# Both 1x1 convolutions of the second stage in the basis where the eight permutations are block diagonal

## The chip, the cores and the metric

The kernel runs on one core of one Trainium2 chip. The metric is the time of the program on the device in microseconds (us), the median of three runs. All arithmetic is in 32-bit floats.

## The reference, cut to what matters

Input x is 16 images of 512 channels, 64 by 64. Layer 0 adds to x a 4x4 blur of its group-normalised self. Layer 1, which the change is about, normalises again and computes an involution with weights that depend on the position:

```python
def d4_1x1(x, w):                       # x: (b, cin*8, h, w), w: (cout, cin, 8)
    W = jnp.stack([w[..., jnp.array(p)] for p in PERMS], axis=1)
    xr = x.reshape(b, cin, 8, h, ww)
    return jnp.einsum('ogif,bifhw->boghw', W, xr).reshape(b, cout * 8, h, ww)

def layer1(x, w_v, w1, gn_gamma, gn_beta, w2, b2):
    t = relu(group_norm(d4_1x1(x, w1), gn_gamma, gn_beta, cmid))     # 512 -> 256 channels
    wgt = einsum('oi,bighw->boghw', w2, t.reshape(b, 32, 8, h, w)) + b2   # 9 taps x 4 groups x 8
    # taps of each of the 8 group elements are rotated or flipped
    xv = d4_1x1(x, w_v)                                              # 512 -> 512 channels
    pats = unfold_patches(xv, 3)                                     # 9 shifted copies
    return (wgt * pats).sum(over the 9 taps)

x = x + layer1(_gn(x), ...)
```

PERMS holds the eight permutations of the symmetries of a square. A layer `d4_1x1` is a full matrix over channels (512 by 512 and 512 by 256), built of 8 by 8 blocks that all have this permutation structure. In a suitable basis of the eight components such a block splits into four one-dimensional parts and two equal 2 by 2 parts.

## The kernel before

The first stage (`stage_a`) blurs all images, writes the sum `x1` to HBM and leaves a scale and a bias per channel and image (`x1_scale`, `x1_bias`). The second stage (`stage_b`) works on one image at a time. Its work order is written out by hand for each engine's queue and joined by semaphores; every queue runs in order.

An image is cut into 4 bands of 16 rows, and these into 4 units of 4 rows. A unit is done in 4 granules of 4 output channels for each of the 32 channel lines, so an image has 16 granules (`N_GRAN`), and `period(i)` walks over them with n = 0 to 15. In granule n:

- DVE multiplies the tap weights of the unit with shifted windows of `val` (`product`): taps 0 to 2 are summed by DVE itself with the residual in `acc` (`opening`, two halves; its last sum is L1015), taps 3 to 8 (`pooled`, products j = 0 to 5, the last two "late", within the next granule's opening) go to `prod_p`, a ring of four.
- POOL adds the six products to `acc`, one after the other (L917). Before a granule's first add it waits for DVE's sums in `acc` (`own`). After granule 13's adds it also does a power for the next image's statistics (`RSTD_AT`).
- SP loads the residual of granule n + 2 and stores `acc` of granule n - 1 once POOL has finished it.
- PE and ACT make `val` for granule n + 3 (`values`, `keep_values`): 1x1 convolution `w_v`, four input blocks (`kt`) by four bands as 32-column matmuls (L672), into a ring of two PSUM banks that ACT empties (`take`).
- At the end of a unit PE computes the tap weights of the next one into five other PSUM banks (`tap_weights`, L686): banks 0 to 2 "EARLY" after step 3, 7 or 11, banks 3 and 4 "LATE" at the start of step 4, 8 or 12. Each bank waits until DVE has read the old weights (`bank_done`), and ACT adds the bias (`tap_bias`, L823) before DVE may use it.

Between these the next image is prepared: SP loads its channels into `xm` (and the last unit into `xs`), ACT normalises them in place (`normalize`, L769), PE convolves them with `w1` in full 128-column matmuls of 512 pixels (`conv_t`, L656, at the steps in `CONV_AT`), ACT keeps the result `t`, DVE takes its statistics (`t_stats`, `t_aggregate`, at granules 6, 8, 10 and 12; `t_spreads`, `t_add_eps` and `t_affine` at 14), and ACT applies them with a relu. `rows_above` and `complete` copy the rows that bands share. After granule 15 comes `lead(i + 1)`: the first values, the relu of unit 0 and its tap weights. For the first image none of this lies under another's pooling; the last image has no next one to prepare (`more=False`).

Of the kernel before, what the change touches and what calls it, by code (L numbers as in the profile page):

```python
# [28 lines left out]
P = 128  # L29
# [61 lines left out]
def program(nc, x, shifts, mean_a, kern, member_of, w1t, wvt, w2t, w2mask, b2t, gamma, beta, mean_b, out, x1):  # L91

    with ExitStack() as top:
# [9 lines left out]
        with ExitStack() as ctx:  # L103
            stage_b(nc, ctx, sem, ps, x1, w1t, wvt, w2t, w2mask, b2t, gamma, beta, mean_b, out, x1_scale, x1_bias)
# [344 lines left out]
def stage_b(nc, ctx, sem, ps, x1, w1t, wvt, w2t, w2mask, b2t, gamma, beta, mean_b, out, x1_scale, x1_bias):  # L449
# [5 lines left out]
    xs = sb("xs", [P, KT, BANDS * UPX])  # L455
# [6 lines left out]
    w1 = sb("w1", [P, KT, CMID])  # L462
    wv = sb("wv", [P, KT, CM * 32])
# [16 lines left out]
    w1_in, const_in = sem("w1_in"), sem("b_const_in")  # L480
# [3 lines left out]
    xm_loaded = [sem(f"xm_loaded{u}") for u in range(UNITS)]  # L484
    xm_ready = sem("xm_ready")
    xs_ready = sem("xs_ready")
    xm_above = sem("xm_above")
    xm_whole = sem("xm_whole")
# [23 lines left out]
    LEAD_MM = 4 * UNITS + sum(V_BANKS[:AHEAD])  # L512
    PERIOD_MM = 4 * UNITS + sum(V_BANKS)

    CONV_AT = {1: (3, 0), 2: (0, 0), 4: (0, 1), 5: (3, 1), 6: (1, 0), 8: (1, 1), 10: (2, 0), 11: (2, 1)}
# [8 lines left out]
    def values_end(i, n, more=True):  # L524

        if n < AHEAD:
            return period_base(i) - sum(V_BANKS[n + 1:AHEAD])
        return period_base(i) + sum(V_BANKS[AHEAD:n + 1]) + \
            (2 * sum(s < n - AHEAD for s in CONV_AT) if more else 0)

    def t_end(i, u):

        if isinstance(i, int) and i == 0:
            return 4 * (u + 1)
        last = max(step for step, (unit, _) in CONV_AT.items() if unit == u)
        return period_base(i) - PERIOD_MM + sum(V_BANKS[AHEAD:last + AHEAD + 1]) + 2 * sum(x <= last for x in CONV_AT)

# [26 lines left out]
    def xs_rows(kt):  # L564
        return xs[:, kt, :].rearrange("p (q n) -> p q n", q=BANDS)
# [4 lines left out]
    def _(sp):  # L570
        def load_xm(i, u):
            if u == UNITS - 1:
                if not first(i):
# [180 lines left out]
    def _(act):  # L754
# [92 lines left out]
        for u in range(UNITS):  # L847
            if u == 0:
                normalize(0, 0)
# [284 lines left out]
```

## Time and profile before

| what | value |
|---|---|
| median of 3 runs | 5242.5 us (5240.94 to 5243.19) |
| the profiled execution, its own time | 5241.05 us |
| its span, first to last instruction | 5239.3 us |
| PE, DVE, ACT, POOL busy, share of the span | 88%, 89%, 45%, 86% |
| mean granted TensorE clock | 0.956 |
| PE in `values` (L672), `conv_t` (L656), tap weights (L686) | 2112.9, 692.8 + 227.9, 570.2 us |
| POOL adds (L917) | 3652.7 us, 1536 of 2378 ns |

"Busy" is the time with an instruction in work on the engine. Matmuls are pipelined, so PE's busy time and the mean of one matmul overstate what a single one costs in a row; the length of a burst divided by its instructions is the better price. An f32 matmul appears as two instructions. The shares are averages over both stages: the first ends near 1087 us. DVE and POOL rows that follow one another overlap by a little, so a row of starts says more than a sum of durations.

### The profile page before, as it was taken

What the parts mean: (1) busy time and instruction counts of PE and PEld (TensorE: products, weight loads), DVE (VectorE), ACT (ScalarE), POOL (GpSimd) and SP (SyncE); (2) the same over time, 40 slices, a digit from 0 to 9 for tenths busy, and PEclk for the clock granted to TensorE, in tenths of its full rate; (3) what the DMA queues carried; (4) which work ended last, traced back from release to release, by engine and by line L of the source; (5) the groups of instructions that cost most, each with busy time, mean ns of one, the idle gap of its engine ahead of it and who ended that gap; (6) DMA issues with size and microseconds to landing.
All of it is one profiled execution on the core that took longest, in us unless ns stands there. A gap on an engine that the chain in (4) does not pass through costs nothing.

```text
span 5239.3 us, 140780 instructions
## 1 busy us (share of the span) xinstructions
PE 4611.1 (88%) x52820; PEld 2173.0 (41%) x52820; DVE 4657.8 (89%) x7999; ACT 2349.3 (45%) x3633; POOL 4515.2 (86%) x2208
## 2 busy tenths in 40 slices
PE   8999999979898989898989898989898988888873
PEld 3333333334443434353435343434344444444342
DVE  6777777727999999999999999999999999999998
ACT  7999999944242333333333333333323233323221
POOL 6888888826998989898989898989898999899999
PEclk9999999989999999999999999999999999999986
DMA  8999999843333333232333333333333232323221
GB/s 237 257 257 257 257 257 257 235 129 103 100 102 101 99 98 115 85 119 91 111 98 103 101 98 102 102 98 102 98 102 114 86 117 83 114 95 109 82 74 57
DMA packets 868592, 681.28 MB, mean 130 GB/s; under 512 B 555840, under 2 KB 818368, under 8 KB 851520
## 3 DMA queue, kind: packets, MB, share of 16 engines
q1 hardware_dynamic: 868032, 673.64, 43.3%
q8 instruction: 373, 6.11, 0.5%
q14 instruction: 187, 1.53, 0.1%
HBM read 405.08 MB, written 268.44 MB: 129 GB/s over the span
## 4 chain that ended last, share of the span: by engine, by line
PE 37%; DVE 19%; issue 12%; POOL 6%; ACT 4%; DVEq 1%; DMA 0%; ACTq 0%; POOLq 0%; SPq 0%
PE ps L672 18%; PE ps L656 13%; PE ps L686 7%; POOL acc L917 6%; DVE prod_p L968 6%; DVE ps L1009 3%; DVE ps L1012 2%; DVE ps L968 2%; DVE acc L1015 2%; DVE prod_d L968 2%; DVE six_t L933 2%; ACT xs L769 1%; ACT t L830 1%; ACT val L817 1%; DVE dev_t L949 1%
## 5 line engine op out<-in xcount | busy, mean ns | idle before, releaser
L917 POOL TENSOR_TENSOR acc<-acc,prod_p 128x1024 f32<-128x1024 f32 x1536 | 3652.7, 2378 | 383.1 <-DVE acc L1015 156.2
L672 PE MATMUL ps<-xm,wv 128*32 128x256 f32 (+1 forms) x32768 | 2112.9, 418 | 121.4 <-ACT val L817 89.8
L968 DVE TENSOR_TENSOR prod_p<-ps,val 128x1024 f32<-128x1024 f32 x1536 | 1858.4, 1217 | 65.8 <-POOL acc L917 63.1
L672 PEld LDWEIGHTS ps<-xm,wv 128*32 128x32 f32 x32768 | 1070.3, 112 | 1165.2 <-issue 557.0
L284 PE MATMUL ps<-xn,band 64*64 64x512 f32 x8192 | 948.2, 598 | 21.5 <-issue 13.9
L817 ACT ACTIVATE val<-ps 128x512 f32<-128x512 f32 (+1 forms) x640 | 345.6, 556 | 1326.7 <-PE ps L672 1038.0
L968 DVE TENSOR_TENSOR prod_d<-ps,val 128x512 f32<-128x512 f32 x1024 | 698.8, 682 | 146.5 <-ACT ps L823 142.5
L656 PE MATMUL ps<-xm,w 128*128 128x512 f32 x1536 | 692.8, 605 | 88.3 <-ACT val L817 69.0
L686 PE MATMUL ps<-t,w 128*32 128x256 f32 x9216 | 570.2, 404 | 227.2 <-ACT t L830 117.6
L316 POOL TENSOR_TENSOR x_out<-x_out,x_in 128x512 f32<-128x512 f32 x512 | 636.2, 1274 | 0.0
L244 ACT ACTIVATE x_out<-ps 64x512 f32<-64x512 f32 x1024 | 606.2, 592 | 50.5 <-PE ps L284 29.1
L686 PEld LDWEIGHTS ps<-t,w 128*32 128x32 f32 x9216 | 302.4, 116 | 496.2 <-DVE ps L1009 117.2
L284 PEld LDWEIGHTS ps<-xn,band 64*64 64x64 f32 x8192 | 326.3, 132 | 432.3 <-issue 428.0
L656 PEld LDWEIGHTS ps<-xm,w 128*128 128x128 f32 x1536 | 287.9, 192 | 457.2 <-issue 377.8
L331 POOL TENSOR_TENSOR rstd<-var_eps,power 128x8 f32 (+2 forms) x133 | 212.9, 1601 | 237.3 <-DVE var_eps L378 237.3
L823 ACT ACTIVATE ps<-ps,b 128x256 f32<-128x256 f32 x576 | 235.1, 443 | 403.5 <-PE ps L686 401.1
L231 ACT ACTIVATE xn<-x_in,norm_b,rstd 128x512 f32<-128x512 f32 x512 | 389.5, 809 | 6.7
L798 ACT ACTIVATE t<-ps 128x512 f32<-128x512 f32 x192 | 114.6, 597 | 563.1 <-PE ps L656 563.1
L1009 DVE TENSOR_TENSOR ps<-ps,acc 128x512 f32<-128x512 f32 x512 | 353.8, 691 | 10.8 <-DMA acc<-x 10.8
L1012 DVE TENSOR_TENSOR ps<-ps,prod_d 128x512 f32<-128x512 f32 x512 | 353.8, 691 | 0.0
L968 DVE TENSOR_TENSOR ps<-ps,val 128x512 f32<-128x512 f32 x512 | 353.7, 691 | 0.0
L1015 DVE TENSOR_TENSOR acc<-ps,prod_d 128x512 f32<-128x512 f32 x512 | 349.4, 682 | 0.0
(59 smaller groups left out, 2366.8 us busy)
## 6 DMA issues: line engine op xcount, KB each, us to landing
x_in<-x SPq DMA_DIRECT2D x128, 1024.0 KB, 7.4
x<-x_out SPq DMA_DIRECT2D x256, 512.0 KB, 5.3
acc<-x SPq DMA_DIRECT2D x1024, 128.0 KB, 2.7
out<-acc SPq DMA_DIRECT2D x256, 512.0 KB, 2.7
xm<-x SPq DMA_DIRECT2D x192, 512.0 KB, 5.9
xs<-x SPq DMA_DIRECT2D x64, 512.0 KB, 6.4
wv<-wvt SPq DMA_DIRECT2D x1, 1024.0 KB, 8.0
w<-w1t SPq DMA_DIRECT2D x1, 512.0 KB, 8.2
```

Source lines behind the costliest of these rows:

```text
L244: nc.scalar.activation(group(x_out[H2 * t:H2 * t + H2, r, :], W, W, 0, 2 * two + x).rearrange("p m h w -> p m (h w)"), ps[at:at + H2, 2 * ...
L284: mm = nc.tensor.matmul(ps[to:to + H2, 2 * two + t, :], band[rows, v, rows], group(xn[rows, k % N_RING, :], XP, W, v, 2 * two + x), start= ...
L316: nc.gpsimd.tensor_tensor(out, out, group(x_in[:, k % X_RING, :], W, W, 0, g) .rearrange("p m h w -> p m (h w)"), ALU.add).then_inc(x_adde ...
L656: mm = nc.tensor.matmul(ps[:, b, :], w1[:, kt, m * P:(m + 1) * P], rows[:, 2 * h:2 * h + 2, :], start=(kt == 0), stop=(kt == KT - 1))
L672: mm = nc.tensor.matmul(ps[32 * q:32 * q + 32, b, at:at + ROWS[u] * W], wv[:, kt, (m + x) * 32:(m + x + 1) * 32], xm[:, kt, r0:r0 + ROWS[u ...
L686: mm = nc.tensor.matmul(taps_of(tap)[32 * q:32 * q + 32, :], w2[:, kt, tap * 32:(tap + 1) * 32], t[:, kt, u, q * UPX:(q + 1) * UPX], start ...
L817: nc.scalar.activation(val[:, m:m + per, lo:lo + ROWS[u], 1:1 + W], src, ACT.Copy) .then_inc(kept, 1)
L917: nc.gpsimd.tensor_tensor(acc[:, r, :], acc[:, r, :], prod_p[:, k % P_RING, :], ALU.add).then_inc(p_added, 1)
L968: return nc.vector.tensor_tensor(dst.rearrange("p (m r w) -> p m r w", m=count, w=W), taps_of(tap).rearrange("p (m r w) -> p m r w", m=1, ...
L1009: nc.vector.tensor_tensor(ps[:, D_BANK, :], ps[:, D_BANK, :], acc[:, r, half], ALU.add).then_inc(own, 1)
L1012: nc.vector.tensor_tensor(ps[:, D_BANK, :], ps[:, D_BANK, :], prod_d[:, 0, :], ALU.add).then_inc(own, 1)
L1015: nc.vector.tensor_tensor(acc[:, r, half], ps[:, D_BANK, :], prod_d[:, 1, :], ALU.add).then_inc(own, 1)
```

## The change

Both convolutions are computed in the basis in which the permutation structure is block diagonal. An image is cut into 8 chunks of 512 pixels (half a unit). For a chunk, `forward` transforms the four input blocks of 128 channels into four `xh` tiles, each of one irreducible part; normalisation is applied when ACT evicts them (`keep_forward`, with a scale and bias carried into the new basis by `affine`). `block_v` and `block_t` multiply with the block matrices `wh` for the two convolutions; their results, still in the new basis, go to `xm` and `t`. `inverse` transforms `t` back, in place; for the other convolution the back transform is what `values` now does, with one matmul per band instead of four. The chunks' steps have tables of their own. Raw input goes to `xr`, a buffer of one chunk. `wh` is built on DVE at the start of the stage. The bands' shared rows are copied by `edges`. DVE's statistics move to granules 5, 8, 11 and 13.

```diff
-LOAD_AT = {1: 0, 5: 1, 9: 2}
-LOAD_LAST_AT = 15
-NORMALIZE_AT = {2: 0, 6: 1, 10: 2}
-ABOVE_AT = 9
+IRR = 4
+CHUNKS, CPX = 8, 512
+OQ = QM + MT
+FORWARD_AT = {0: 0, 1: 1, 2: 2, 4: 3, 6: 4, 7: 5, 8: 6, 9: 7}
+BLOCK_V_AT = {1: 0, 2: 1, 4: 2, 5: 3, 8: 4, 9: 5, 12: 6, 13: 7}
+BLOCK_T_AT = {1: (0,), 2: (1,), 4: (2,), 5: (3,), 8: (4,), 9: (5,), 10: (6, 7)}
+INVERSE_AT = {1: (0,), 2: (1,), 4: (2,), 5: (3,), 8: (4,), 9: (5,), 11: (6, 7)}
+LOAD_AT = {1: 1, 2: 2, 3: 3, 5: 4, 7: 5, 8: 6, 9: 7}
+LOAD_NEXT_AT = 10
+EDGES_AT = 13
 RSTD_AT = (13, 5)
-WHOLE = 2
+EDGES = 2
 SETUP = 4
...
     block = ctx.enter_context(nc.Block())
...
-        def load_xm(i, u):
...
-                wait_apart(sp, sp_apart, mm_full, values_end(i - 1, GRANS * u + GRANS - 1))
+        def load_x(i, c):
+
+            if not (first(i) and c == 0):
+                prev = (i, c - 1) if c > 0 else (i - 1, CHUNKS - 1)
+                wait_apart(sp, sp_apart, mm_full, chunk_end(prev[0], "forward", prev[1]))
...
+                sp.dma_start(xr[:, kt, :].rearrange("p (q n) -> p q n", q=2), src).then_inc(x_loaded, 16)

...
+        sp.dma_start(base[:], basis).then_inc(base_in, 16)
+        load_x(0, 0)
+        sp.dma_start(w_src, wsrc).then_inc(w_in, 16)
+        sp.dma_start(w_sign, signs).then_inc(w_in, 16)
+        for dst, src in ((w2, w2t), (blk, mean_b), (b2, b2t), (gam, gamma), (bet, beta)):
             sp.dma_start(dst[:], src).then_inc(const_in, 16)
         sp.dma_start(mask, w2mask).then_inc(const_in, 16)
...
+        for c in range(1, CHUNKS):
+            load_x(0, c)
         load_resid(0, 0)
         load_resid(0, 1)
-        load_xm(1, UNITS - 1)
+        load_x(1, 0)

...
                 if more and n in LOAD_AT:
-                    load_xm(i + 1, LOAD_AT[n])
-                if ahead and n == LOAD_LAST_AT:
-                    load_xm(i + 2, UNITS - 1)
+                    load_x(i + 1, LOAD_AT[n])
+                if ahead and n == LOAD_NEXT_AT:
+                    load_x(i + 2, 0)
...
-        def conv_t(i, u, halves):
...
+        def affine():
+
+            for kt in range(KT):
+                q = slice(32 * kt, 32 * kt + 32)
+                nc.tensor.matmul(ps[q, D_BANK, 0:B], first_of,
+                                 x1_scale[:].rearrange("p (b k) -> p k b", k=KT)[:, kt, :], start=True, stop=True,
+                                 skip_group_check=True)
+                for r in range(IRR):
+                    mm = nc.tensor.matmul(ps[q, D_BANK, (1 + r) * B:(2 + r) * B], forward_m[:, r, :],
+                                          x1_bias[:].rearrange("p (b k) -> p k b", k=KT)[:, kt, :],
+                                          start=True, stop=True, skip_group_check=True)
+            mm.then_inc(affine_mm, 1)
+
+        def forward(i, c):
+
+            pe.wait_ge(x_loaded, i * (16 * KT * CHUNKS) + 16 * KT * (c + 1))
+            for r in range(IRR):
+                b = take()
+                for kt in range(KT):
+                    mm = nc.tensor.matmul(ps[32 * kt:32 * kt + 32, b, :], forward_m[:, r, :], xr[:, kt, :],
+                                          start=True, stop=True, skip_group_check=True)
+                mm.then_inc(mm_full, 1)
+
+        def block_of(i, c, outputs):
+
+            pe.wait_ge(kept, chunk_end(i, "forward", c))
+            for o in outputs:
+                b = take()
+                for r in range(IRR):
+                    mm = nc.tensor.matmul(ps[32 * r:32 * r + 32, b, :], wh[:, r, o, :], xh[:, c % 2, r, :],
+                                          start=True, stop=True, skip_group_check=True)
+                mm.then_inc(mm_full, 1)
+
+        def block_v(i, c):
+            block_of(i, c, range(QM))
+
+        def block_t(i, c):
+            block_of(i, c, range(QM, OQ))
+
+        def inverse(i, c):
+
+            pe.wait_ge(kept, chunk_end(i, "block_t", c))
+            for m in range(MT):
+                b = take()
+                nc.tensor.matmul(ps[:, b, :], inverse_t, t_chunk(m, c), start=True, stop=True).then_inc(mm_full, 1)

         def values(n, halves=(0, 1)):

-            u, m0 = n // GRANS, n % GRANS * QM
+            u, q4 = n // GRANS, n % GRANS
             per = QM // V_BANKS[n]
-            for m in range(m0 + halves[0] * QM // 2, m0 + (halves[-1] + 1) * QM // 2, per):
+            for m in range(halves[0] * QM // 2, (halves[-1] + 1) * QM // 2, per):
                 b = take()
                 for x in range(per):

                     row, at = (0 if u == 0 else u * UR + 2), x * ROWS[u] * W
-                    for kt in range(KT):
-                        for q in range(BANDS):
-                            r0 = (q * BR + row) * W
-                            mm = nc.tensor.matmul(ps[32 * q:32 * q + 32, b, at:at + ROWS[u] * W],
-                                                  wv[:, kt, (m + x) * 32:(m + x + 1) * 32],
-                                                  xm[:, kt, r0:r0 + ROWS[u] * W],
-                                                  start=(kt == 0), stop=(kt == KT - 1), skip_group_check=True)
+                    for q in range(BANDS):
+                        r0 = (q * BR + row) * W
+                        mm = nc.tensor.matmul(ps[32 * q:32 * q + 32, b, at:at + ROWS[u] * W],
+                                              inverse_v[:, m + x, :], xm[:, q4, r0:r0 + ROWS[u] * W],
+                                              start=True, stop=True, skip_group_check=True)
                 mm.then_inc(mm_full, 1)
...
-            pe.wait_ge(xm_above, i + 1)
+            pe.wait_ge(xm_edges, EDGES * (i + 1))
...
+        pe.wait_ge(base_in, 16)
+        affine()
+        forward(0, 0)
+        pe.wait_ge(w_built, 1)
+        for c in range(CHUNKS):
+            block_v(0, c)
+            block_t(0, c)
+            if c < CHUNKS - 1:
+                forward(0, c + 1)
+            inverse(0, c)
+        pe.wait_ge(const_in, 16 * 6)
...
             for n in range(N_GRAN):
                 if n > 0 and n % GRANS == 0:
                     tap_weights(i, n // GRANS, LATE)
-                if n + AHEAD == 2 * GRANS:
-                    pe.wait_ge(xm_whole, WHOLE * (i + 1))
                 if n + AHEAD < N_GRAN:
                     values(n + AHEAD)
-                if more and n in CONV_AT:
-                    u, half = CONV_AT[n]
-                    conv_t(i + 1, u, [half])
+                if more:
+                    if n in BLOCK_V_AT:
+                        block_v(i + 1, BLOCK_V_AT[n])
+                    for c in BLOCK_T_AT.get(n, ()):
+                        block_t(i + 1, c)
+                    if n in FORWARD_AT:
+                        forward(i + 1, FORWARD_AT[n])
+                    for c in INVERSE_AT.get(n, ()):
+                        inverse(i + 1, c)
                 if n % GRANS == GRANS - 1 and n < N_GRAN - 1:
                     tap_weights(i, n // GRANS + 1, EARLY)
             if more:
...
+        def keep_forward(i, c):
+
+            for r in range(IRR):
+                b = take(apart=True)
+                nc.scalar.activation(xh[:, c % 2, r, :], ps[:, b, :], ACT.Identity,
+                                     bias=xh_affine[:, 1 + r, bass.ds(i, 1)],
+                                     scale=xh_affine[:, 0, bass.ds(i, 1)]).then_inc(kept, 1)
+
+        def keep_block_v(i, c):
+
+            for q4 in range(QM):
+                b = take()
+                nc.scalar.activation(xm_chunk(q4, c), ps[:, b, :].rearrange("p (q n) -> p q n", q=2), ACT.Copy)\
+                    .then_inc(kept, 1)
+
+        def keep_block_t(i, c):
+
+            if c >= CHUNKS - 2 and not first(i):
+                act.wait_ge(t_ready, i * (MT * UNITS))
+            for m in range(MT):
+                b = take()
+                nc.scalar.activation(t_chunk(m, c), ps[:, b, :], ACT.Copy).then_inc(kept, 1)
+
+        def keep_inverse(i, c):
+
+            for m in range(MT):
+                b = take()
+                nc.scalar.activation(t_chunk(m, c), ps[:, b, :], ACT.Copy).then_inc(kept, 1)
+
+        def edges(i):
...
             if not first(i):
                 act.wait_ge(mm_full, values_end(i - 1, N_GRAN - 1))
...
+            act.wait_ge(kept, chunk_end(i, "block_v", CHUNKS - 1))
+            nc.scalar.activation(bands[:, :, 1:, 0:W], bands[:, :, 0:BANDS - 1, (BR - 2) * W:(BR - 1) * W], ACT.Copy)\
+                .then_inc(xm_edges, 1)
+            nc.scalar.activation(bands[:, :, 0:BANDS - 1, (BR - 1) * W:], bands[:, :, 1:, W:2 * W], ACT.Copy)\
+                .then_inc(xm_edges, 1)
...
-            keep_t(0, u, range(MT))
-            if u == UNITS - 2:
-                rows_above(0)
+        act.wait_ge(affine_mm, 1)
+        nc.scalar.activation(xh_affine[:], ps[:, D_BANK, 0:(1 + IRR) * B].rearrange("p (e b) -> p e b", b=B), ACT.Copy)\
+            .then_inc(affine_kept, 1)
+        act.wait_ge(affine_kept, 1)
+        keep_forward(0, 0)
+        for c in range(CHUNKS):
+            keep_block_v(0, c)
+            keep_block_t(0, c)
...
                 t_add_eps(i + 1)
             pooled(i, n, 2)
-            if more and n == 6:
+            if more and n == 5:
                 t_stats(i + 1, 0)
             if more and n == 8:
+                t_stats(i + 1, 1)
+            if more and n == 11:
+                t_stats(i + 1, 2)
+            pooled(i, n, 3)
+            if more and n == 13:
                 t_stats(i + 1, 3)
-            if more and n == 10:
-                t_stats(i + 1, 1)
-            pooled(i, n, 3)
-            if more and n == 12:
-                t_stats(i + 1, 2)
                 t_aggregate(i + 1)
             if more and n == 14:
                 t_affine(i + 1)
...
-        dve.wait_ge(const_in, 16 * 7)
+        dve.wait_ge(w_in, 32)
+        w_sum = ps[:, 0:2, 0:4 * OQ * 16].rearrange("p b (c o) -> p b c o", c=4)
+        for j in range(GR):
+            if j > 1:
+                dve.wait_ge(w_chain, 2 * j - 1)
+            coeff = w_src[:, j, :].rearrange("p (b c o) -> p b c o", b=1, c=1).to_broadcast([P, 2, 4, OQ * 16])
+            sign = w_sign[:, j].rearrange("p b (c o) -> p b c o", o=1).to_broadcast([P, 2, 4, OQ * 16])
+            nc.vector.tensor_tensor(w_term if j > 0 else w_sum, coeff, sign, ALU.mult).then_inc(w_chain, 1)
+            if 0 < j < GR - 1:
+                dve.wait_ge(w_chain, 2 * j)
+                nc.vector.tensor_tensor(w_sum, w_sum, w_term, ALU.add).then_inc(w_chain, 1)
+        dve.wait_ge(w_chain, 2 * GR - 2)
+        for b in range(2):
+            for e in range(2):
+                def part(a):
+                    return a[:, b].rearrange("p (r e) (q o) -> p r e q o", e=2, o=16)[:, :, e]
+                last = nc.vector.tensor_tensor(wh[:, 2 * b:2 * b + 2, :, 16 * e:16 * e + 16],
+                                               part(w_sum), part(w_term), ALU.add)
+        last.then_inc(w_built, 1)
+        dve.wait_ge(const_in, 16 * 6)
```

Left out of the diff: names of semaphores and tiles, the index helpers that count the order of the ring (`chunk_end` gives the number of evictions up to the end of a chunk's step), and the host's preparation of the transform matrices, the signs and the coefficients `wsrc`.

## Rows read from the trace of the kernel before

**Rows 1.** Windows: busy us (instructions) of PE, PEld, DVE, ACT, POOL; granted clock, DMA
```profile
2241.60:2494.10 252.50, 222.58 (x2758) 109.72 (x2757) 241.18 (x316) 84.65 (x131) 230.14 (x98) 0.96 0.32 102
2450.50:2458.40 7.90, 7.67 (x100) 3.92 (x104) 7.59 (x10) 1.73 (x5) 5.83 (x3) 0.69 0.25 89
5018.80:5239.30 220.50, 109.91 (x1700) 63.13 (x1688) 191.70 (x244) 28.62 (x57) 204.60 (x87) 0.74 0.18 63
```

**Rows 2.** Waits in one image: engine, waited for, us, times, longest
```profile
DVE prod_d L968 <- ACT ps L823: 7.8, 6, 3.7
...
POOL acc L917 <- DVE acc L1015: 8.0, 4, 2.3
...
DVE prod_p L968 <- POOL acc L917: 3.0, 3, 1.1
```

**Rows 3.** Waits of DVE in the last image, all of them
```profile
DVE prod_p L968 <- POOL acc L917: 16.8, 16, 1.3
```

**Rows 4.** DVE timeline at granule 4: start, us, instruction, idle before
```profile
2268.07 0.69 DVE L968 TENSOR_TENSOR prod_d<-ps,val 128x512 f32<-128x512 f32 x1 [3.70 <-ACT ps L823]
...
2269.79 0.69 DVE L968 TENSOR_TENSOR prod_d<-ps,val 128x512 f32<-128x512 f32 x1 [0.43 <-ACT ps L823]
```

**Rows 5.** POOL timeline of one image, the adds after its longest waits
```profile
2280.61 105.82 POOL L917 TENSOR_TENSOR acc<-acc,prod_p 128x1024 f32<-128x1024 f32 x42 [2.34 <-DVE acc L1015]
...
2436.51 0.71 POOL L904 TENSOR_TENSOR rstd_t<-var_eps_t,power_b 128x2 f32<-128x2 f32 x1 [1.19 <-DVE var_eps_t L955]
...
2454.03 75.65 POOL L917 TENSOR_TENSOR acc<-acc,prod_p 128x1024 f32<-128x1024 f32 x30 [1.93 <-DVE acc L1015]
```

**Rows 6.** POOL timeline of the last image: six adds a granule
```profile
5025.26 14.88 POOL L917 TENSOR_TENSOR acc<-acc,prod_p 128x1024 f32<-128x1024 f32 x6 [0.17 <-POOL acc L917]
...
5055.43 15.04 POOL L917 TENSOR_TENSOR acc<-acc,prod_p 128x1024 f32<-128x1024 f32 x6 [0.17 <-POOL acc L917]
...
5221.32 14.77 POOL L917 TENSOR_TENSOR acc<-acc,prod_p 128x1024 f32<-128x1024 f32 x6 [0.17 <-POOL acc L917]
```

**Rows 7.** Chain that ended last, one image: PE bursts and small DVE work
```profile
2244.28 7.04 PE ps L672 x128
2251.32 7.06 PE ps L656 x16
...
2405.37 2.39 DVE six_t L933 x4
...
2428.40 1.93 DVE dev_t L949
```

**Rows 8.** Lines of one image by form: ACT rows and one DVE row
```profile
L968 DVE TENSOR_TENSOR prod_p<-ps,val 128x1024 f32<-128x1024 f32 x97 | 117.4, 1217 | 3.2 <-POOL acc L917 3.0
...
L769 ACT ACTIVATE xm<-xm,x_bias,x_scale 128x1024 f32<-128x1024 f32 x12 | 13.9, 1232 | 0.0
...
L798 ACT ACTIVATE t<-ps 128x512 f32<-128x512 f32 x12 | 7.2, 598 | 35.6 <-PE ps L656 35.6
...
L789 ACT ACTIVATE xm<-xs 128x4096 f32<-128x4096 f32 x1 | 3.6, 3614 | 0.0
```

**Rows 9.** Lines of the whole run: ACT normalisation of the first stage
```profile
L231 ACT ACTIVATE xn<-x_in,norm_b,rstd 128x512 f32<-128x512 f32 x512 | 389.5, 809 | 6.7
```

**Rows 10.** Chain that ended last, start of the second stage
```profile
1089.20 7.50 DMA xm<-x
...
1101.58 57.92 PE ps L656 x128
1159.50 10.46 PE ps L672 x128
...
1175.46 9.60 PE ps L686 x144
```

**Rows 11.** POOL timeline of the first image: granules 0 and 4
```profile
1190.36 15.01 POOL L917 TENSOR_TENSOR acc<-acc,prod_p 128x1024 f32<-128x1024 f32 x6 [17.94 <-DVE acc L1015]
...
1274.88 15.00 POOL L917 TENSOR_TENSOR acc<-acc,prod_p 128x1024 f32<-128x1024 f32 x6 [3.24 <-DVE acc L1015]
```

More of the change, by code:

```diff
@@ L511, in stage_b, with order_of_period, order_at_first, ends @@
     EARLY, LATE = (0, 1, 2), (3, 4)
-    LEAD_MM = 4 * UNITS + sum(V_BANKS[:AHEAD])
-    PERIOD_MM = 4 * UNITS + sum(V_BANKS)
-    CONV_AT = {1: (3, 0), 2: (0, 0), 4: (0, 1), 5: (3, 1), 6: (1, 0), 8: (1, 1), 10: (2, 0), 11: (2, 1)}
+    LEAD = sum(V_BANKS[:AHEAD])
+    def order_of_period(more):
+        for n in range(N_GRAN):
+            if n + AHEAD < N_GRAN:
+                yield ("values", n + AHEAD), V_BANKS[n + AHEAD]
+            if more:
+                if n in BLOCK_V_AT:
+                    yield ("block_v", BLOCK_V_AT[n]), QM
+                for c in BLOCK_T_AT.get(n, ()):
+                    yield ("block_t", c), MT
+                if n in FORWARD_AT:
+                    yield ("forward", FORWARD_AT[n]), IRR
+                for c in INVERSE_AT.get(n, ()):
+                    yield ("inverse", c), MT
+    def order_at_first():
+        yield ("forward", 0), IRR
+        for c in range(CHUNKS):
+            yield ("block_v", c), QM
+            yield ("block_t", c), MT
+            if c < CHUNKS - 1:
+                yield ("forward", c + 1), IRR
+            yield ("inverse", c), MT
+    def ends(order):
+        total, at = 0, {}
+        for what, n in order:
+            total += n
+            at[what] = total
+        return at, total
+    IN_PERIOD, PERIOD_MM = ends(order_of_period(True))
+    IN_LAST, _ = ends(order_of_period(False))
+    AT_FIRST, FIRST_MM = ends(order_at_first())
+    LEAD_MM = FIRST_MM + LEAD
+    PERIOD_MM += LEAD
     def taps_of(tap):
@@ L527, in values_end, with chunk_end @@
             return period_base(i) - sum(V_BANKS[n + 1:AHEAD])
-        return period_base(i) + sum(V_BANKS[AHEAD:n + 1]) + \
-            (2 * sum(s < n - AHEAD for s in CONV_AT) if more else 0)
+        return period_base(i) + (IN_PERIOD if more else IN_LAST)["values", n]
+    def chunk_end(i, what, c):
+        if isinstance(i, int) and i == 0:
+            return AT_FIRST[what, c]
+        return period_base(i) - PERIOD_MM + IN_PERIOD[what, c]
     def t_end(i, u):
[L533 to L536, printed above, removed]
+        return chunk_end(i, "inverse", 2 * u + 1)
     def p_done(i, n, j):
@@ L762, in take @@
             return b
-        def normalize(i, u):
-            wait_apart(act, act_apart, xm_loaded[u], (i + 1) * (16 * KT))
-            for kt in range(KT):
-                v, done = (xs_rows(kt), xs_ready) if u == UNITS - 1 else (xm_rows(kt, u), xm_ready)
-                nc.scalar.activation(v, v, ACT.Identity, bias=x1_bias[:, bass.ds(i * KT + kt, 1)],
-                                     scale=x1_scale[:, bass.ds(i * KT + kt, 1)]).then_inc(done, 1)
-        bands = xm[:].rearrange("p k (q n) -> p k q n", q=BANDS)
@@ L860, in _ @@
         keep_values(0, 2)
-        complete(0)
         relu(0, 1)
```

164 lines of the change are left out of this document (76 added, 88 removed).

## The prediction

> **What bounds the kernel now.** I read the windows first. Of one image in the middle (252.5 us) VectorE (DVE) is busy 241.2, GpSimd (POOL) 230.1, TensorE (PE) 222.6, ScalarE (ACT) 84.7 [rows 1]. Three engines are near full, so shares decide nothing; the waits do. DVE waits in that image 7.8 us for ACT's bias on the tap weights and 3.0 us for POOL's adds, and for nothing else of size [rows 2]. The first sort is where PE matters: the tap weights of the next unit are queued on PE behind `values` and `conv_t`, and at granule 4 DVE stands still 3.70 us and then 0.43 us for them [rows 4].
>
> Next, what DVE would be held by if those waits went. POOL's 230 us understate it: its adds are chained, 42 of them take 105.82 us from first to last, so 2.52 us each and 15.12 us a granule of six [rows 5]. DVE's own work in a plain granule is shorter. The last image shows it: it has no convolutions of a next image, its granules follow each other at 15.08 us ((5221.32 - 5025.26) / 13) [rows 6], DVE never waits for ACT and waits 16.8 us in all for POOL, about 1.05 a granule [rows 3]. So DVE needs about 14.0 us, and POOL sets the pace wherever DVE is not held up. Sixteen granules at 15.12 are 241.9 us; that is the floor an image can come near. The time between the S4 marks (the first add of granule 4) of the first and last image is 5055.43 - 1274.88 over 15 images, 252.04 us each [rows 6, 11]. About 10 us an image are on offer, of which PE's lateness is only a part: POOL runs dry four times (8.0 us in all) waiting for DVE's sums [rows 2], 2.34 at granule 4 and 1.93 at granule 15, so 3.8 between, in granules 12 and 13, and 1.19 more at the small `rstd_t` power [rows 5]. Granule 15's is the price of DVE's small statistics operations, not of PE.
>
> **PE's part.** A 128x128 instruction of 512 columns takes 0.441 us (7.06 / 16), an instruction of a 32-column group with 256 columns 0.055 (7.04 / 128) [rows 7]; an f32 matmul is two instructions, so four 32-column groups of 512 columns, or one full matmul of 512, are 0.88 us. Per image that removes `conv_t` (128 instructions, 56.5 us) and three quarters of `values` (2048 instructions down to 512; of about 126 us, at 0.055 and 0.082 each [rows 7, 10], some 95 go). It adds 32 forward, 32 `block_v`, 16 `block_t` and 16 `inverse` fills of 0.88, 84.7 us. PE falls from 222.6 to about 156 us. For the four groups running together with 512 columns the rows of 256 speak; if they ran only two at a time a fill would be 1.76.
>
> **ACT's part.** Removed: 16 normalisations of 1.23 (19.7 us), the copy of 3.6 and two small ones, about 25 us. Added: 32 forward evictions with scale and bias, not seen before from PSUM: between 0.60 (a plain eviction [rows 8]) and 0.81 (scale and bias, SBUF to SBUF [rows 9]); I take 0.75, nearer the form with both pointers, 24 us. Then 32 `block_v` and 16 `block_t` evictions at 0.60, 29 us, and two edge copies of about 0.8. ACT goes from 85 to about 115 us (bounds 110 to 117): not a bound. PE fills one bank (0.88) while ACT empties the other (0.60 to 0.75), so the ring runs at PE's pace.
>
> **Does the new order keep the tap weights in time?** Of DVE's 14.0 us in a granule six products take about 1.13 each back to back (1.217 less their overlap [rows 8]), so the twelve short operations 0.6. `val` of granule n - 1 is thus free 5.2 us into granule n (five short ones and two late products), and there ACT's step n begins. A full step (1, 2, 4, 8, 9) has 14 fills or fewer, 12 of them 0.88, about 13 us with a halo copy; it ends before the next step opens. Steps 3, 7 and 11, which end in the early tap weights, hold two values fills and none, four or four chunk fills: PE is through at about 7, 10.5 and 10.5 us. Bank 0 is released by DVE at 7.1 (three short ones more); its 32 instructions (1.76) and two biases end near 10, 13 and 13 us, before granule end at 15.1. So the waits at granules 4, 8 and 12 go; a small one stays at granule 0, behind the relu. Loads: `xr` is a single buffer, a chunk's load starts when the forward of the chunk before is done and SP has stored the granule before. For chunk 5 that puts landing (at most 7.5 us, the row of the first load [rows 10]) about 6 us into granule 7, where PE wants it; PE waits in order, so lateness there moves the tap weights behind it, but some 2 us are covered by slack. Residual loads and stores queue behind SP's new waits; they are needed a granule later.
>
> **DVE's part in the loop.** The same four statistics groups (2.39 us each [rows 7]) move; the last, with its aggregation, comes in granule 13, directly before the small operations of 14, one of which takes 1.93 [rows 7]. DVE can be behind POOL's pace by what the wait of 4.13 us at granule 4 cost POOL less: 4.13 - 2.34, 1.8 us [rows 4, 5]. After the group of granule 11 that cover is 1.8 + 1.05 - 2.39 = 0.5; one plain granule makes it 1.5; then granule 13's 3.0 and the first small operations' 2.2 against another 1.05 leave POOL dry by 2.7 us, plus 0.8 for the power behind it. Granule 15's 1.93 stays (1.8 beyond the usual hand-over). New image: 241.9 + 3.5 + 1.8 = 247.2 us, against 252.04: 4.8 saved. For leftovers of tap waits I give back 0.5: 4.3 x 15 = 65 us.
>
> **The start.** No chunk work hides behind pooling in the first image. Before, convolutions take 57.92 us from 1101.58, `values` 10.46, statistics and relu up to 1175.46 [rows 10]. After: sources of the block matrices land near 1100; DVE builds them in 14 chained operations of 768 elements, about 0.95 each (a product of 1024 takes 1.22 [rows 8]) and four short ones, to about 1115.5. Then 92 fills at 0.88 with some hand-over, 84 us, to 1199.5; edges 1.7; `values(0)` a quarter, 2.6; the same 5.5 us of statistics and relu: tap weights start at 1209.5, 34 us later. POOL's first add moves from 1190.36 to 1224. From there granules run at 15.1, since the residual load that had to wait behind a load for image 1 no longer does, and no convolution delays granule 4: S4 comes at 1284.7 instead of 1274.88 [rows 11]. Net cost 10 us.
>
> **Sum.** 5239.3 + 10 - 65 = 5184 us of span; the profiled run has 1.75 us outside its span and lies 1.5 below the median, so 5187; I state 5185.
>
> **The rivals.** (1) PE's lower clock, slower than before. In the stretch 2450.5 to 2458.4, behind a wait for ACT, the granted clock is 0.69, a mean of 1.2 and 2.4 GHz, and the 96 tap instructions cost 7.67 us of PE instead of 5.3 [rows 1, 7]. With PE idle a third of the time, steps 7 and 11 open cold; if their four fills (7.0 us from 6.4) and the taps (3.5 a bank) run at 1.2 GHz, bank 0 is ready at 17.8 us and bank 1 at 21.3, and DVE waits 5.0 us at granule 8 and 3.7 at 12. By the same cover sum an image loses 8.1 and takes 255.3: 5239 + 10 + 49, about 5298. It decides from about 3.5 us of wait at each. Against it: in the last image the clock is 0.74 and DVE waits for no bias at all [rows 1, 3]. The Trainium skill speaks for this rival: "TensorE: Matmul & The Clock Gate", HAM oscillation, says that pauses between bursts put the array back to half clock, so fewer matmuls need not be less time; the row at 0.69 agrees. (2) Half of that: only step 11's lateness counts, about 2.5 us an image back: 5184 + 30, 5215. A late chunk load gives about the same. (3) Fill and eviction do not overlap, 1.2 us a fill: start 92 x 0.32 = 29 us longer, 5215 with a little from heavy steps running over. The skill's "TensorEngine Tiling (Array Packing)", PSUM Bottleneck, warns of it: packing speeds up the array, not the emptying of PSUM. Evictions of 0.60 against fills of 0.88 say no. (4) The change doesn't save: POOL and DVE trade waits as before, the image stays at 252, and the start costs its 10: 5251.
>
> **How the numbers follow.** Forecast 0.60; (1) 0.08; (2) 0.14; (3) 0.10; (4) 0.08. 0.2% (10.5 us) is about what a measurement of this kernel tells from no change. Faster: the forecast, (2) and (3) less a small part, 0.81; same: (4) mostly, 0.09; slower: (1) and the rest, 0.10. The forecast's own range is 5150 (all tap waits gone, starving 1.5 us less than worked out, start 10 cheaper) to 5205; the range that takes in (2) and (3) goes to 5238.
>
> **What would show it.** In the profile after: PE near 156 us an image, ACT near 115; DVE's waits for the bias under 2 us an image and those for POOL up from 3 to about 7; the granules 15.1 apart except at 13 to 15; POOL's first add near 1224. Wrong would be: bias waits at granules 8 or 12 with the clock low; PE waiting for chunk loads in the loop; a chunk at the start far from 10.6 us; or POOL's adds slower than 2.52 us.

## The result, and the profile after

The changed kernel takes 5194.8 us (median of four runs, 5193.2 to 5196.2) against 5242.8 for the kernel before on the same chip: a ratio of 0.9909, 95% interval 0.9892 to 0.9926. The forecast was 5185, with 5150 to 5205 as its own range and 5238 as the end of the range that takes in rivals (2) and (3). The profiled execution has a span of 5193.5 us.

First the page after, the busy shares and the chain that ended last by engine, and below them that chain in the kernel before.

```profile
PE 3796.5 (73%) x36988; PEld 1315.4 (25%) x36988; DVE 4670.5 (90%) x8017; ACT 2854.0 (55%) x4642; POOL 4507.4 (87%) x2208
...
POOL 51%; DVE 13%; issue 9%; PE 4%; POOLq 1%; ACT 1%; DMA 0%; DVEq 0%; SPq 0%; ACTq 0%
```

```profile
PE 37%; DVE 19%; issue 12%; POOL 6%; ACT 4%; DVEq 1%; DMA 0%; ACTq 0%; POOLq 0%; SPq 0%
```

PE has gone from 88% of the span to 73%, but the shares of DVE and POOL are nearly what they were. What changed is the chain: half of it is now POOL's adds, and PE has 4% for 37%. Before, it ran through PE's bursts behind `values` and `conv_t` again and again [rows 7].

A window as the first of [rows 1], one image in the middle of the run:

```profile
1979.10:2226.90 247.80, 174.75 (x1764) 56.39 (x1764) 239.32 (x313) 115.92 (x194) 228.13 (x97) 0.86 0.33 103
```

The image has 1764 PE instructions for 2758, PE is busy 175 us for 223, ACT 116 for 85, and the granted clock fell from 0.96 to 0.86.

The waits of DVE and of POOL over the fifteen steady images (1230 to 5000 us), against those of [rows 2]:

```profile
DVE prod_p L1078 <- POOL acc L1027: 96.4, 109, 1.2
DVE prod_d L1078 <- ACT ps L929: 16.5, 32, 1.0
...
POOL rstd_t L1014 <- DVE var_eps_t L1065: 55.5, 15, 3.7
POOL acc L1027 <- DVE acc L1125: 50.4, 22, 18.1
```

DVE's wait for the bias on the tap weights is 1.1 us an image (16.5 / 15), from 7.8; no single one is longer than 1.0. Its waits for POOL have risen from 3.0 to 6.4 (96.4 / 15). POOL's own long waits are now two an image, 3.70 before the power and 1.94 before granule 15, which its timeline shows (start, duration, instruction, idle before):

```profile
1230.01 14.96 POOL L1027 TENSOR_TENSOR acc<-acc,prod_p 128x1024 f32<-128x1024 f32 x6 [18.07 <-DVE acc L1125]
...
1290.77 15.00 POOL L1027 TENSOR_TENSOR acc<-acc,prod_p 128x1024 f32<-128x1024 f32 x6 [0.17 <-POOL acc L1027]
...
2141.15 45.05 POOL L1027 TENSOR_TENSOR acc<-acc,prod_p 128x1024 f32<-128x1024 f32 x18 [0.23 <-POOL acc L1027]
2189.91 0.71 POOL L1014 TENSOR_TENSOR rstd_t<-var_eps_t,power_b 128x2 f32<-128x2 f32 x1 [3.70 <-DVE var_eps_t L1065]
2190.59 14.82 POOL L1027 TENSOR_TENSOR acc<-acc,prod_p 128x1024 f32<-128x1024 f32 x6
2207.35 181.35 POOL L1027 TENSOR_TENSOR acc<-acc,prod_p 128x1024 f32<-128x1024 f32 x72 [1.94 <-DVE acc L1125]
...
5010.19 14.86 POOL L1027 TENSOR_TENSOR acc<-acc,prod_p 128x1024 f32<-128x1024 f32 x6 [0.17 <-POOL acc L1027]
```

The hole of 2.34 us at granule 4 [rows 5] is gone: 72 adds, twelve granules, run without a stop at 2.52 us each (181.35 / 72). The S4 marks are 1290.77 and 5010.19, so an image takes 247.96 us (before 252.04). The books close: 15 x 4.08 = 61.2 us saved in the images, 15.9 lost before the first mark (1290.77 - 1274.88), and behind the last mark 183.3 us for 183.9. Together 5239.3 - 61.2 + 15.9 - 0.6 = 5193.4, the span.

Where the 15.9 come from, the chain at the start of the second stage shows (start, duration, what):

```profile
1109.67 1.16 DVE wh L1177 x4
1110.87 8.08 PE ps L732 x48
...
1125.03 5.51 PE ps L732 x48
1130.54 1.04 PE ps L722 x8
1131.69 0.79 ACT xh L871
1132.52 1.11 PE ps L722 x8
...
1134.66 1.96 PE ps L747 x4
1136.62 5.51 PE ps L732 x48
...
1205.12 4.37 PE ps L760 x32
...
1214.99 5.20 PE ps L773 x57
```

`wh` is built by 1110.87, and eight chunks take 92.5 us to the last eviction at 1203.40. A chunk is 11.59 us (1136.62 - 1125.03): six block fills in 5.51, the four forward fills with two of their evictions on the path, two inverse fills. Tap weights start at 1214.99 instead of 1175.46 [rows 10], POOL's first add at 1230.01 instead of 1190.36 [rows 11]; 24 of the 40 us come back by the S4 mark, since nothing holds granules 0 to 4 up any more.

### The profile page after: what moved, and what is told of

It is laid out like the page before. It is cut to its first block, busy times and chain, and to the rows that moved or that the text cites. A ratio compares the mean times of both kernels' runs of the same rounds, so it can differ in the third digit from the quotient of the medians.

```text
span 5193.5 us, 113938 instructions
## 1 busy us (share of the span) xinstructions
PE 3796.5 (73%) x36988; PEld 1315.4 (25%) x36988; DVE 4670.5 (90%) x8017; ACT 2854.0 (55%) x4642; POOL 4507.4 (87%) x2208
## 4 chain that ended last, share of the span: by engine, by line
POOL 51%; DVE 13%; issue 9%; PE 4%; POOLq 1%; ACT 1%; DMA 0%; DVEq 0%; SPq 0%; ACTq 0%
POOL acc L1027 51%; DVE prod_p L1078 3%; DVE ps L1122 2%; DVE ps L1119 2%; DVE ps L1078 1%; DVE six_t L1043 1%; DVE acc L1125 1%; DVE prod_d L1078 1%; PE ps L722 1%; PE ps L732 1%; PE ps L773 1%; DVE dev_t L1059 1%; POOLq L1024 1%; DMA xr<-x 0%; POOLq L1026 0%
## 5 line engine op out<-in xcount | busy, mean ns | idle before, releaser
L773 PE MATMUL ps<-t,w 128*32 128x256 f32 x9216 | 614.0, 425 | 435.7 <-ACT t L936 225.5
L760 PE MATMUL ps<-xm,base 128*32 128x256 f32 (+1 forms) x8192 | 636.2, 445 | 166.4 <-ACT val L923 73.7
L732 PE MATMUL ps<-xh,wh 128*32 128x512 f32 x6144 | 706.8, 600 | 49.6 <-ACT val L923 33.7
L722 PE MATMUL ps<-xr,base 128*32 128x512 f32 x4096 | 547.1, 659 | 213.3 <-ACT val L923 124.1
L871 ACT ACTIVATE xh<-ps,xh_affine 128x512 f32<-128x512 f32 x512 | 395.1, 777 | 195.5 <-PE ps L722 180.0
L879 ACT ACTIVATE xm<-ps 128x512 f32<-128x512 f32 x512 | 306.0, 598 | 190.4 <-PE ps L732 190.4
L760 PEld LDWEIGHTS ps<-xm,base 128*32 128x32 f32 x8192 | 251.2, 115 | 563.8 <-issue 186.4
L916 ACT ACTIVATE val<-val 128x512 f32<-128x512 f32 x192 | 120.5, 628 | 436.7 <-DVE prod_p L1078 436.6
```

Of the source, the lines that this page charges most:

```text
L722: mm = nc.tensor.matmul(ps[32 * kt:32 * kt + 32, b, :], forward_m[:, r, :], xr[:, kt, :], start=True, stop=True, skip_group_check=True)
L732: mm = nc.tensor.matmul(ps[32 * r:32 * r + 32, b, :], wh[:, r, o, :], xh[:, c % 2, r, :], start=True, stop=True, skip_group_check=True)
L760: mm = nc.tensor.matmul(ps[32 * q:32 * q + 32, b, at:at + ROWS[u] * W], inverse_v[:, m + x, :], xm[:, q4, r0:r0 + ROWS[u] * W], start=True ...
L773: mm = nc.tensor.matmul(taps_of(tap)[32 * q:32 * q + 32, :], w2[:, kt, tap * 32:(tap + 1) * 32], t[:, kt, u, q * UPX:(q + 1) * UPX], start ...
L871: nc.scalar.activation(xh[:, c % 2, r, :], ps[:, b, :], ACT.Identity, bias=xh_affine[:, 1 + r, bass.ds(i, 1)], scale=xh_affine[:, 0, bass. ...
```

## The experiments

The theory: the images gain because PE is no longer late with the tap weights, after which POOL's chained adds set the pace. Rivals: PE's lateness only changes places with POOL's waits; the lower clock takes the gain back; the gain is that of the moved statistics on DVE.

**Less PE work in the kernel before.** It leaves out three of the four input blocks of `values`, and nothing else: no transform, no moved statistics, no longer start.

```diff
-                    for kt in range(KT):
+                    for kt in range(1):
...
-                                                  start=(kt == 0), stop=(kt == KT - 1), skip_group_check=True)
+                                                  start=True, stop=True, skip_group_check=True)
```

> The kernel before, with the value convolution over the first of its four input blocks only (three of four blocks are left out, so 95 us less of PE an image and nothing else changed). Theory A, PE's lateness at the tap weights: DVE's waits for the bias fall from 9.0 us an image to under 1.5, POOL paces the loop, an image takes 246 to 248 us instead of 252.0, and the whole about 5150 us. Theory B, the gain came from the rest of the rearrangement (statistics moved, loads, evictions): within 0.2% of the kernel before, 5243. Theory C, a less busy PE drops to its lower clock and is late all the same: bias waits stay above 5 us an image and the time above 5215.

Measured: 5188.2 us, ratio 0.9893 (0.9876 to 0.9909): less than expected, and not where it was expected. The profiled span is 51.8 us shorter (5187.5 for 5239.3). About half of that, 24.9, lies ahead of the S4 mark of the first image (1249.93 for 1274.88): from 1175 to 1280 DVE waits 7.9 us for ACT and the residual's load instead of 35.5. The S4 marks then follow at 250.28 us instead of 252.04, 26 us over the run. POOL's timeline shows what became of its stops, and below it stands one stretch of the kernel before:

```profile
1675.32 180.56 POOL L917 TENSOR_TENSOR acc<-acc,prod_p 128x1024 f32<-128x1024 f32 x72 [1.93 <-DVE acc L1015]
...
1874.48 14.85 POOL L917 TENSOR_TENSOR acc<-acc,prod_p 128x1024 f32<-128x1024 f32 x6 [3.38 <-DVE acc L1015]
```

```profile
1448.25 181.54 POOL L917 TENSOR_TENSOR acc<-acc,prod_p 128x1024 f32<-128x1024 f32 x72 [1.76 <-DVE acc L1015]
```

The hole at granule 4 is gone in every image behind the first, but there is now one of 3.3 to 3.4 us at granule 12 of every image but the last, where the kernel before mostly has 1.7. POOL's waits come to 142.1 us from 1300 to 4900, against 144.9 before, so in the loop the lateness has moved more than it has gone. Most of the 26 us is POOL's pace instead: 72 adds in a row take 180.56 us for 181.54, which makes 1.3 us an image. Why the adds are a little faster with less work on PE, no run shows.

At granule 12 the clock bites. DVE's timeline at granule 12 (start, duration, instruction, idle before), and the chain of the same stretch:

```profile
2113.09 0.69 DVE L968 TENSOR_TENSOR prod_d<-ps,val 128x512 f32<-128x512 f32 x1 [5.64 <-ACT ps L823]
```

```profile
2100.17 10.14 PE ps L656 x16
```

In the kernel before, the same convolution of 16 instructions takes 7.06 us when PE is kept busy ahead of it [rows 7]. At the place shown it takes 7.13 there, behind a pause of PE of 2.15 us. Here the pause, in which PE waited for ACT's `val`, is 4.7 us, the granted clock from 2100 to 2112 is 0.74, a mean of 1.2 and 2.4 GHz, and the burst takes 10.14. The wait at granule 12 is then 5.64 us where the kernel before has 2.63. The waits for the bias fell only to 5.6 us an image (81.2 us from 1300 to 4900, for 117.8 before).

**The PE work put back into the changed kernel.** `values` does its matmuls three times, with the same result.

```diff
-                    for q in range(BANDS):
+                    for q in list(range(BANDS)) * 3:
```

> The changed kernel, with each matmul of the values done three times over (same result; about 63 us of PE an image added, which brings PE back to some 220 us, the load of before). Theory A: the tap weights are late again, bias waits of several us an image, an image takes 250 to 254 us instead of 248.0, the whole 5230 to 5290. Theory B: nothing changes, 5195.

Measured: 5300.8 us, ratio 1.0112 (1.0095 to 1.0129), slower than the kernel before. PE is busy 221.6 us of an image of 253.5 and the clock is back at 0.97. Behind the first image DVE waits 113.9 us for the bias (1330 to 4900), and POOL's hole at granule 4 is back in every image but the last:

```profile
2317.72 4.94 POOL L1027 TENSOR_TENSOR acc<-acc,prod_p 128x1024 f32<-128x1024 f32 x2 [0.95 <-DVE prod_p L1078]
2326.03 75.71 POOL L1027 TENSOR_TENSOR acc<-acc,prod_p 128x1024 f32<-128x1024 f32 x30 [3.37 <-DVE acc L1125]
```

The image is as the theory expected, and makes 84 of the 106 us over the changed kernel (15 times 253.54 - 247.96). The total is above the expectation, because POOL stood still 19 us more at granule 4 of the first image (15.89 and 3.25). PE at full clock and late costs more here than PE at 0.86 and in time.

**The statistics put back to granules 6, 8, 10 and 12** (the four numbers in `period` alone).

> The changed kernel, with DVE's statistics at granules 6, 8, 10 and 12 as in the kernel before. Theory A with the cover of 1.8 us: POOL runs dry by 0.1 us at granule 11, 1.0 at 13, 1.2 and the power at 14, 1.8 at 15; about half a microsecond an image less than now, 5187 us, within 15 of the changed kernel. Theory B, the moved statistics saved the time: 2 us an image or more given back, 5225 or above.

Measured: 5211.3 us, ratio 0.9939 (0.9923 to 0.9956), between the two expectations, and neither holds. The image is 249.2 us. Of the 48 us that the change gained, 16.5 hang on where the statistics are and about 32 on the rest; neither alone is the cause. POOL's timeline shows where, at granules 9 and 13, each right behind a group of statistics:

```profile
2363.07 29.98 POOL L1027 TENSOR_TENSOR acc<-acc,prod_p 128x1024 f32<-128x1024 f32 x12 [1.32 <-DVE acc L1125]
...
2426.10 14.84 POOL L1027 TENSOR_TENSOR acc<-acc,prod_p 128x1024 f32<-128x1024 f32 x6 [2.11 <-DVE acc L1125]
```

The expectation had no stop at granule 9 and 1.0 us at 13. The places also act on the tap weights: DVE's waits for the bias are 54.0 us (1300 to 4900), where the changed kernel has 16.5. So the two causes are not cleanly apart in this run.

**The statistics in halves.** If a group of 2.39 us is too much for the 1.05 us that DVE has over in a granule, two groups of half the size in neighbouring granules should let it keep up.

```diff
+STATS_AT = {5: (0, [0]), 6: (0, [1]), 7: (1, [0]), 8: (1, [1]), 10: (2, [0]), 11: (2, [1]), 12: (3, [0]), 13: (3, [1])}
...
+            if more and n in STATS_AT:
+                t_stats(i + 1, *STATS_AT[n])
```

> The changed kernel, with each unit's statistics cut in two halves in neighbouring granules (5 to 8 and 10 to 13), the aggregation at 13. Theory A with the cover of 1.8 us: a half costs 1.2 us where a granule gives back 1.05, so POOL reaches granule 14 with cover left; its wait there falls from 3.7 us to about 1.4, an image to 245.3 us, the whole to 5155 to 5165. If POOL's pace alone sets the loop, or its waits don't come from DVE's work in granules 11 to 13: no change, 5195.

Measured: 5151.5 us, ratio 0.9826 (0.981 to 0.9842), the image 245.2, both close to what was expected. POOL's wait at the power falls from 3.70 to 1.19; the one at granule 15 stays at 1.94.

**And DVE's small operations with an operand in PSUM.** What stays is the 1.19 and 1.94, and both follow operations on two numbers a partition (`dev_t`, `t_bias`) that take 2 us. In the changed kernel's rows by form, in the middle of the run:

```profile
L1074 DVE TENSOR_TENSOR t_bias<-bet,dev_t 128x2 f32<-128x2 f32 x1 | 2.3, 2257 | 0.0
L1059 DVE TENSOR_TENSOR dev_t<-dev_t 128x2 f32<-128x2 f32 x1 | 2.0, 1957 | 0.0
L1070 DVE TENSOR_TENSOR t_scale<-rstd_t,gam 128x2 f32<-128x2 f32 x1 | 0.9, 941 | 0.0
...
L1072 DVE TENSOR_TENSOR dev_t<-t_scale,ps 128x2 f32<-128x2 f32 x1 | 0.2, 156 | 0.0
```

The fast one reads PSUM, the slow ones SBUF alone. The edit keeps the deviation, its square and the product for the bias in a free corner of the PSUM bank that `opening` uses; for that it computes the deviation twice and waits for DVE's own sums. The diff is cut to two of the operations:

```diff
-            nc.vector.tensor_tensor(dev[:], dev[:], dev[:], ALU.mult).then_inc(t_chain, 1)
+            nc.vector.tensor_tensor(square_ps, dev_ps, dev[:], ALU.mult).then_inc(t_chain, 1)
...
-            nc.vector.tensor_tensor(t_bias[:], bet[:], dev[:], ALU.subtract).then_inc(t_norm, 1)
+            nc.vector.tensor_tensor(t_bias[:], bet[:], dev_ps, ALU.subtract).then_inc(t_norm, 1)
```

> The changed kernel with the split statistics of the run before, and two of DVE's three slow small operations at granule 14 given an operand in PSUM instead of SBUF only. Theory D: a small DVE operation whose operands all lie in SBUF waits until POOL's running add ends; then the square of 1.96 us and the bias of 2.26 us fall to about 0.2 each, POOL's waits at granules 14 and 15 (1.2 and 1.9 us) go, an image takes 242.5 us and the whole about 5112 us. Rival: these operations are slow for another reason, keep their time, and the whole stays at 5151.

Measured: 5114.5 us, ratio 0.9756 (0.974 to 0.9773), the image 242.84 (S4 marks at 1292.13 and 4934.73), as theory D expected: the best version of this study, faster than both kernels. The same rows, and POOL's timeline:

```profile
L1066 DVE TENSOR_TENSOR ps<-ps,dev_t 128x2 f32<-128x2 f32 x1 | 0.2, 168 | 0.0
...
L1082 DVE TENSOR_TENSOR t_bias<-bet,ps 128x2 f32<-128x2 f32 x1 | 0.2, 157 | 0.0
```

```profile
2204.53 166.26 POOL L1028 TENSOR_TENSOR acc<-acc,prod_p 128x1024 f32<-128x1024 f32 x66 [0.59 <-DVE acc L1134]
2371.01 45.13 POOL L1028 TENSOR_TENSOR acc<-acc,prod_p 128x1024 f32<-128x1024 f32 x18 [0.23 <-POOL acc L1028]
2416.40 0.71 POOL L1015 TENSOR_TENSOR rstd_t<-var_eps_t,power_b 128x2 f32<-128x2 f32 x1 [0.25 <-DVE var_eps_t L1073]
```

**Both DVE edits in the kernel before,** with PE's work as it was (the aggregation moves from granule 12 to 13).

> The kernel before with DVE's part of both runs alone: its statistics in halves at granules 6 to 13, the small operations by PSUM; PE's work as it was. Theory A: PE's lateness at granules 4 and 12 remains (DVE waits about 9 us an image for the bias, POOL runs dry some 2.3 and 1.3 us there), DVE's share of POOL's dry time goes; an image takes about 246.6 us, the whole 5155 to 5170. If PE's lateness were all that held the kernel before: no change, 5243. If DVE's own work were all: the time of the changed kernel with the same edits, less its longer start, near 5100.

Measured: 5153.8 us, ratio 0.9831 (0.9814 to 0.9847). The two small edits gain more on the old kernel (88 us) than the change of the convolutions (48). On top of them the change still brings 39 (5153.8 to 5114.5), so DVE's side work was not all that held the kernel before. With PE's work left in, DVE waits 93.1 us for the bias (1300 to 4900; 26.8 in the changed kernel with the same edits), and POOL has a hole of over 2 us at granule 4 in five of the fourteen images between the first and the last, here one of them:

```profile
2268.65 105.75 POOL L918 TENSOR_TENSOR acc<-acc,prod_p 128x1024 f32<-128x1024 f32 x42 [3.38 <-DVE acc L1024]
```

**A plain forward eviction.** It leaves out the scale and bias of the normalisation, to price the start's chunk.

```diff
-                nc.scalar.activation(xh[:, c % 2, r, :], ps[:, b, :], ACT.Identity,
-                                     bias=xh_affine[:, 1 + r, bass.ds(i, 1)],
-                                     scale=xh_affine[:, 0, bass.ds(i, 1)]).then_inc(kept, 1)
+                nc.scalar.activation(xh[:, c % 2, r, :], ps[:, b, :], ACT.Copy).then_inc(kept, 1)
```

> The changed kernel, with the forward evictions as plain copies (the scale and the bias of the normalisation are left out). Theory E: in the first image a forward's four fills wait for evictions of 0.78 us in the ring of two banks; with 0.60 they don't, a chunk takes 11.1 us instead of 11.6, POOL's first add comes about 4 us earlier, and the loop doesn't change. Rival: the fills themselves take 1.04 us, the chunk stays at 11.6.

Measured: 5189.6 us in a single run. The chain at the start:

```profile
1109.31 7.61 PE ps L732 x48
...
1122.63 5.51 PE ps L732 x48
1128.14 3.73 PE ps L722 x32
...
1131.90 1.96 PE ps L747 x4
1133.86 5.51 PE ps L732 x48
...
1144.65 6.12 DMA xr<-x
```

The evictions are off the chain and the chunk is 11.23 us instead of 11.59: of the 1.0 us above the forecast's 10.6 they are a third. The rest is the fills themselves, 0.92 to 0.98 us each (5.51 / 6, 3.73 / 4, 1.96 / 2) with PE at its upper level, a granted clock of 1.00, in that stretch of the changed kernel (1130.54 to 1190.47); 0.88 was taken. A faster chunk also runs into its load, which takes part of the gain back: the eight chunks take 91.0 us for 92.5. POOL's first add came 2.8 us earlier, at 1227.22, but 1.6 of that was there before the first chunk's block fills (1109.31 for 1110.87).

## Why the prediction was right, and where its sizes were off

**What bounds the kernel.** Right: with PE in time, POOL's adds set the pace at 2.52 us each, and the granules follow at 15.1. The lateness of the tap weights is shown as a cause by the PE work put back: bias waits, the hole at granule 4 and 5.6 us an image came back with it. Less PE work alone, in the kernel before, gave the image only 1.8 us, most of it by POOL's faster adds; there the waits did mostly change places, as rival (4) says. For the changed kernel that rival is refuted: POOL's waits are 87.3 us from 1300 to 4900 where the kernel before has 144.9. That granule 12 is in time as well follows from its trace, but no run takes apart which part of the new order does it.

**Where POOL runs dry.** Right in place, nearly in size, and that in part by luck. At granule 14, 2.7 + 0.8 = 3.5 us were forecast; the gap beyond the usual hand-over is 4.2 (2190.59 - 2186.20 - 0.17). At granule 15 it is 1.8, as forecast (1.94 - 0.17). With the floor of 241.9 that is 247.9, the measured image but for 0.06. The 0.5 given back for late tap weights came to less than that: the image shown here has one hole of 0.71 at granule 9, the next none. So 0.7 too little at granule 14 and most of the 0.5 cancel, and the image was mis-sized by 0.26 us (247.96 for 247.7), 4 us in all. The account behind the 3.5, that DVE can be 1.8 us behind before POOL runs dry, did not hold with the statistics at their old places: there it gave 5187, and 5211.3 was measured, with waits for the bias that it left out. What the cover really is, no run measures.

**ACT and PE.** ACT's 115 us came out as 115.9, the forward eviction at 0.777 us for the 0.75 taken. PE is busy 175 us, not 156. Busy overstates, and the clock was lower; the two can't be told apart here. Neither made DVE wait more than 1.1 us an image for the bias.

**The start** is the term that was off most: the S4 mark at 1290.77 for 1284.7, 6.1 us. `wh` was ready 4.6 us sooner than worked out, mostly because DVE could begin at 1095.85 and not near 1100. Against that, eight chunks cost 92.5 us instead of 84: 2.6 in the first burst, which followed a pause of PE and took 8.08 us at a granted clock of 0.67 where later ones take 5.51; the rest in fills of 0.92 to 0.98 and the exposed evictions. `values(0)` took 4.37 us for 2.6: the clock is 0.63 there, and four short fills run one after another with their evictions. So rival (3) holds in a small part (0.36 us a chunk by the plain eviction). The Trainium skill, "TensorEngine Tiling (Array Packing)", PSUM Bottleneck, warns that packing speeds up the array and not the emptying of PSUM, and the trace agrees in that part: a bank's round of fill, eviction and hand-over takes 1.98 us (1132.52 - 1130.54), so a ring of two gives 0.99 a forward fill, where the packed matmuls alone take 0.93 (3.73 / 4 in the run with plain evictions).

Between the span forecast, 5184, and the 5193.5 measured, 6.1 us are the start and 3.8 the images; 0.6 came back behind the last mark, which the forecast left as it was. The total that the sum led to was 5187, of which 5185 was stated; that takes the forecast 2 us further from 5194.8.

**The clock, rivals (1) and (2).** The mechanism is there, the price is not. In the changed kernel the last unit's inverse, behind a wait of PE for `val` at step 11, takes 896 ns an instruction at a granted clock of 0.63 (2381.61 to 2387.46), and the others 619 (rows by form, 2207.35 to 2455.13):

```profile
L747 PE MATMUL ps<-t,base 128*128 128x512 f32 x24 | 11.9, 619 | 1.8 <-ACT t L888 0.8 <-ACT xh L871 0.4
L747 PE MATMUL ps<-t_last,base 128*128 128x512 f32 x8 | 5.8, 896 | 9.1 <-ACT val L923 9.1
```

But only four fills stand before the tap weights, and no wait for the bias is over 1.0 us. In the kernel before with less PE work, 16 slower instructions stand there, and DVE's wait at granule 12 is 3 us longer. The Trainium skill, "TensorE: Matmul & The Clock Gate", HAM oscillation, says that a burst behind a long pause starts at half clock. The trace agrees in both kernels: with fewer matmuls the mean clock of an image went from 0.96 to 0.86 and 0.78.

**PE and its loads.** PE did wait for chunk loads in the loop, 46.6 us in seven waits of up to 8.2 (1230 to 5000), which the prediction named as something that would make it wrong. It didn't: no wait for the bias grew from it.

## What to carry to other kernels

Price an engine's pace by the starts of its chained work (POOL 15.12 us a granule), not by its busy time: that pace times the granules is the floor, and only the holes above it are on offer. Between two engines of nearly the same pace a lump of side work costs about what it exceeds the slack of a step by, so cut it to the size of the slack and look at its smallest operations; here that gained 80 us on top of the change. Work taken off PE lowered its clock here, so what counts is whether the short bursts that others wait for still end in time. And split the gain of a test run by place before calling it proof: half of what less PE work gained in the kernel before lay in the first image, and most of the rest in POOL's pace.

## What the runs showed of the hardware

While POOL adds in SBUF, a DVE operation on two elements a partition whose inputs both lie in SBUF ends with POOL's running add. In the changed kernel DVE's timeline, and below it POOL's, whose rows are cut off by their windows after the first or the second add of six:

```profile
2181.76 1.96 DVE L1059 TENSOR_TENSOR dev_t<-dev_t 128x2 f32<-128x2 f32 x1
...
2192.01 0.94 DVE L1070 TENSOR_TENSOR t_scale<-rstd_t,gam 128x2 f32<-128x2 f32 x1
...
2193.17 2.26 DVE L1074 TENSOR_TENSOR t_bias<-bet,dev_t 128x2 f32<-128x2 f32 x1
```

```profile
2181.36 2.34 POOL L1027 TENSOR_TENSOR acc<-acc,prod_p 128x1024 f32<-128x1024 f32 x1
...
2190.59 2.35 POOL L1027 TENSOR_TENSOR acc<-acc,prod_p 128x1024 f32<-128x1024 f32 x1
...
2190.59 4.83 POOL L1027 TENSOR_TENSOR acc<-acc,prod_p 128x1024 f32<-128x1024 f32 x2
```

`dev_t` ends at 2183.72 and POOL's add at 2183.70; `t_scale` at 2192.95 and 2192.94; `t_bias` at 2195.43 and 2195.42. In all fifteen images whose statistics are taken beside POOL's adds the two ends lie within 0.02 us of each other, for all three operations. `spread_t`, right behind `dev_t` with both inputs in SBUF, takes 0.16 us: it starts at 2183.75, in the hand-over to POOL's next add. With POOL idle in the first image they take 160 ns, and with an operand in PSUM 157 to 168 beside POOL's adds. The trace counts the wait as DVE's busy time, so no view of waits shows it. The Trainium skill has the rule in "SBUF — State Buffer", SBUF: two separate sides: a DVE operation with two SBUF inputs and a GpSimd operation that reads SBUF exclude each other for the whole instruction. The trace agrees: `t_bias` takes 2.26 us beside POOL's adds and 0.16 without them. The prediction took the 1.93 us from its row [rows 7] without asking why two numbers should take so long.
